# A state-space convolution kernel: table doublings on PSUM operands, tables laid out channel-innermost, K's operands turned first, and half of the first Toeplitz products ahead of the loop

## The reference

```
dtA = A * dt[:, None]                       # A = -exp(log_A_real) + 1j*A_imag, 64 modes per channel
Cs  = Cc * (exp(dtA) - 1.0) / A
K   = 2.0 * einsum('hn,hnl->hl', Cs, exp(dtA[:, :, None] * arange(2048))).real
mask = arange(2048) < length[:, None]
u_m = x * mask
y   = causal_convolution(u_m, K) + u_m * D[:, None]
out = x + y * mask
```

## Time and profile before

| what | value |
|---|---|
| median of 3 runs | 881.8 us (881.62 to 883.14) |
| the profiled execution's own time | 882.78 us |
| its span in the trace | 880.9 us |
| PE busy | 828.1 us, 94% |
| DVE busy | 755.0 us, 86% |
| POOL busy | 636.9 us, 72% |
| ACT busy | 624.6 us, 71% |
| mean DMA rate | 172 GB/s |

### The profile page before, as it was taken

One profiled execution on the slowest core, in us unless ns is written; L12 is line 12 of the kernel. 1 busy time (PEld: TensorE's weight loads), 2 busy tenths in 40 slices (PEclk: granted clock), 3 DMA queues, 4 the chain that ended last, 5 costly groups with the idle time before them and its releaser, 6 DMA issues.

```text
span 880.9 us, 22605 instructions
## 1 busy us (share of the span) xinstructions
PE 828.1 (94%) x6218; PEld 760.6 (86%) x6218; DVE 755.0 (86%) x2054; ACT 624.6 (71%) x1710; POOL 636.9 (72%) x692
## 2 busy tenths in 40 slices
PE   0377999999999999999999999999999999999997
PEld 0366988999988999999999999999999999999996
DVE  8976988888888888888888888888888888888886
ACT  2095767776767777777777777777777777777774
POOL 3727877777777877777787777777777778777771
PEclk9789999999999999999999999999999999999999
DMA  3002677777777777777777777777777777777775
GB/s 83 0 1 49 175 177 191 186 196 177 192 179 188 189 191 186 197 185 196 185 196 187 190 192 186 196 185 195 187 195 189 189 190 188 192 189 197 190 197 132
DMA packets 160947, 151.66 MB, mean 172 GB/s; under 512 B 13216, under 2 KB 160928, under 8 KB 160928
## 3 DMA queue, kind: packets, MB, share of 16 engines
q1 hardware_dynamic: 160928, 151.43, 67.8%
HBM read 84.08 MB, written 67.30 MB: 172 GB/s over the span
## 4 chain that ended last, share of the span: by engine, by line
PE 83%; DVE 5%; DMA 5%; ACT 2%; SPq 2%; POOL 1%; issue 1%; POOLq 0%; DVEq 0%
PE y L830 13%; PE y L832 13%; PE y L831 12%; PE y L865 12%; PE v L847 10%; PE xt_even L818 6%; PE xt_odd L818 6%; DMA xall<-in_x_dram 5%; PE v L830 3%; PE v L831 3%; PE v L832 3%; PE y L825 1%; PE y L826 1%; SPq L301 1%; ACT W L441 1%
## 5 line engine op out<-in xcount | busy, mean ns | idle before, releaser
L441 ACT ACTIVATE room<-v 64x192 f32<-64x192 f32 (+1 forms) x768 | 235.8, 307 | 173.6 <-DVE v L738 157.1
L738 DVE SCALAR_TENSOR_TENSOR v<-v,RV,mid 128x192 f32<-128x192 f32 (+2 forms) x512 | 192.4, 376 | 57.2 <-DVE mid L738 2.7
L738 DVE SCALAR_TENSOR_TENSOR mid<-room,RV,v 128x192 f32<-128x192 f32 (+2 forms) x512 | 184.2, 360 | 41.7 <-ACT room L441 22.2
L830 PE MATMUL y<-thi,uhi 128*128 128x256 f32 x512 | 186.4, 364 | 0.2 <-POOL tlo L409 0.2
L734 DVE COPY_PREDICATED xall<-mask,y 128x512 f32<-128x512 int32 x256 | 176.0, 736 | 1.4 <-issue 1.4
L830 PE MATMUL y<-fhi,zhi 128*128 128x256 f32 x512 | 154.6, 302 | 0.8 <-DVE zlo L564 0.7
L421 POOL TENSOR_TENSOR room<-W,B 128x512 f32 (+1 forms) x128 | 135.8, 1061 | 13.7 <-DVE W L708 13.6
L832 PE MATMUL y<-thi,ulo 128*128 128x256 f32 x512 | 144.5, 282 | 0.0
L832 PE MATMUL y<-fhi,zlo 128*128 128x256 f32 x512 | 144.0, 281 | 0.0
L831 PE MATMUL y<-tlo,uhi 128*128 128x256 f32 x512 | 144.0, 281 | 0.0
L831 PE MATMUL y<-flo,zhi 128*128 128x256 f32 x512 | 144.0, 281 | 0.0
(11 more groups left out here) (174 smaller groups left out, 1981.0 us busy)
## 6 DMA issues: line engine op xcount, KB each, us to landing
xall<-in_x_dram SPq DMA_DIRECT2D x256, 256.0 KB, 4.6
out_dram<-xall SPq DMA_DIRECT2D x254, 256.0 KB, 3.4
traw<-krows SPq DMA_DIRECT2D x128, 128.0 KB, 3.0
out_dram<-xall SPq DMA_DIRECT2D x4, 128.0 KB, 2.4
krows<-ksb SPq DMA_DIRECT2D x8, 16.0 KB, 1.8
cin<-in_L_cond_C_dram SPq DMA_DIRECT2D x1, 64.0 KB, 2.0
dall<-in_L_cond_D_dram SPq DMA_DIRECT2D x1, 64.0 KB, 2.4
krows<-zpad SPq DMA_DIRECT2D x1, 63.5 KB, 6.3
```

What stands on the lines that cost most here:

```text
L441: return act.activation(dst, src, ACT.Copy)
L738: return dve.scalar_tensor_tensor(out=out, in0=src, scalar=RV[:, h, k:k + 1], in1=other, op0=ALU.mult, op1=ALU.add)
L830: pe.matmul(o, a_hi, b_hi, start=start, stop=False, skip_group_check=True)
```

## The change

It touches the prologue, the layout of the tables and the first slot.

- `W1`, `W2`, `B1`, `B2`, `bsel` and `RV` become channel-innermost ([128, 16, 128] per plane). PSUM copies into them are contiguous; POOL's reads of them in the loop, for one channel at a time, have a step of 512 bytes. `Yk` is a new channel-first copy of the Y plane for K's products, turned in 4 extra steps.
- DVE's doublings take the powers from `turns`, a PSUM region that ACT fills (two copies), and two of the four temporaries are the PSUM banks `xt[0]` and `xt[1]`. `x_low(0, 0)` moves ahead of DVE's series, because `xt[0]` has to be free. `BANKS` becomes 5.
- The duplicates of NB's planes are copied by POOL instead of ACT.
- `STEPS` has K's operands first, then K, then B, X and R. D is added to K ahead of DVE's own table copies, and ACT's `NR` copies come behind its other table copies.
- ACT does `t_high(0)` first, DVE forms `tlo` of channel 0, and PE does the Toeplitz products of chunks 0 and 1 of channel 0 ahead of `turn_e(0)`. POOL's `t_low(0)` and those products in slot 0 go.

The core of the diff:

```diff
-BANKS = 6
+BANKS = 5
+STEPS = [("bsel", 8), ("bsel", 12), ("Yk", 8), ("Yk", 12), ("Y2", 8), ("Y2", 12), ("Y1", 8), ("Y1", 12),
+         ("Yk", 0), ("Yk", 4), ("bsel", 0), ("bsel", 4), ("Y1", 0), ("Y1", 4), ("Y2", 0), ("Y2", 4),
+         ("K", 0), ("K", 4), ("K", 8), ("K", 12),
+         ("B1", 8), ("B1", 12), ("B2", 8), ("B2", 12), ("B1", 0), ("B1", 4), ("B2", 0), ("B2", 4),
+         ("X1", 8), ("X1", 12), ("X2", 8), ("X2", 12), ("X1", 0), ("X1", 4), ("X2", 0), ("X2", 4), ("R", 0), ("R", 4)]
+BY_VECTOR = [STEPS.index(k) for k in [("B2", 4), ("X1", 12), ("X2", 12), ("X1", 4),
+                                          ("X2", 4), ("R", 0), ("R", 4)]]
...
-        W1 = sb("W1", [P, 2, H, SQ])
+        W1 = sb("W1", [P, 2, SQ, H])
...
+        turns = yb[1][1][:, 0:2 * 4 * N].rearrange("p (c k n) -> p c k n", c=2, n=N)
...
+            for n in range(2):
+                pool.tensor_copy(NB[:, half(n), 0, :], NB[:, half(n), 1, :]).then_inc(s_bdup, 1)
+                pool.tensor_copy(NB[:, half(n), 3, :], NB[:, half(n), 2, :]).then_inc(s_bdup, 1)
...
-                w1 = W1[:, :, h].unsqueeze(3).broadcast_to([P, 2, SQ, SQ])
+                w1 = W1[:, :, :, h].unsqueeze(3).broadcast_to([P, 2, SQ, SQ])
-                b1 = B1[:, h].unsqueeze(1).unsqueeze(1).broadcast_to([P, 2, SQ, SQ])
+                b1 = B1[:, :, h].unsqueeze(1).unsqueeze(1).broadcast_to([P, 2, SQ, SQ])
...
-                if exists(g, j, -2):
+                if exists(g, j, -2) and exists(g, j, -3):
                     t_low(*on(g, j, -2))
...
+            copy(turns[:, 0], lre[:, A_POW:A_POW + 4, :])
+            copy(turns[:, 1], lim[:, A_POW:A_POW + 4, :]).then_inc(s_turns, 1)
...
+            t_high(0, 0)
             e_high(0, 0)
...
+            x_low(0, 0)
             series(q, k, r, k)
...
-            temps = [q1, q2, q3, q4]
-            link(level(dve, link, NY, 1, 0, A_POW, temps, 0))
+            temps = [xt[0], q2, xt[1], q4]
+            coarse = [(turns[:, 0, k], turns[:, 1, k]) for k in range(4)]
+            link(level(dve, link, NY, 1, 0, coarse[0], temps, 0))
...
+            for t in range(T_K, T_K + 4):
+                dve.wait_ge(s_free[t % BANKS], t // BANKS + 1)
+            dve.tensor_tensor(k0, k0, dall[:].rearrange("p (g c) -> p g c", c=8), ALU.add).then_inc(s_kfin, 1)
+
+            for t in BY_VECTOR:
                 filled(dve, t)
                 dve.tensor_copy(place(t), four(t)).then_inc(s_free[t % BANKS], 1)
...
+            dve.wait_ge(s_thi, 1)
+            less(tlo[0][:], traw[0][:, ::-1], thi[0][:]).then_inc(s_tlo0, 1)
...
+                               Yk[:, 8 * g:8 * g + 8, :].rearrange("p c i -> p (c i)"),
+                               bsel[:, :, 8 * g:8 * g + 8].rearrange("p i c -> p c i"), start=True, stop=True)
...
+            for c in range(2):
+                toep_even(0, 0, c)
+                toep_odd(0, 0, c)
             turn_e(0, 0)
```

More of the change, by code:

```diff
@@ L87, in s4d_kernel @@
         q4 = sb("q4", [P, NPOW * N])
-        RV = sb("RV", [P, H, 8])
-        bsel = sb("bsel", [P, H, SQ])
+        RV = sb("RV", [P, 8, H])
+        bsel = sb("bsel", [P, SQ, H])
         tick = sb("tick", [P, 2])
@@ L166, in s4d_kernel @@
         s_nxp = sem("s_nxp")
+        s_turns = sem("s_turns")
+        s_tlo0 = sem("s_tlo0")
         s_yneg = sem("s_yneg")
@@ L247, in half, with level @@
             return slice(SQ // 2, SQ) if n == 0 else slice(0, SQ // 2)
-        def level(eng, link, table, re, im, first, temps, k, lo=0, hi=N):
+        def level(eng, link, table, re, im, turn, temps, k, lo=0, hi=N):
             m = 2 ** k
             old, new = slice(SQ - m, SQ), slice(SQ - 2 * m, SQ - m)
-            c, s = (t[:, first + k, lo:hi].unsqueeze(1).broadcast_to([P, m, hi - lo]) for t in (lre, lim))
+            c, s = (t[:, lo:hi].unsqueeze(1).broadcast_to([P, m, hi - lo]) for t in turn)
             rc, is_, rs, ic = (t[:, 0:(hi - lo) * m].rearrange("p (m n) -> p m n", m=m) for t in temps)
@@ L277, in place @@
                 return ksb[:, i:i + 4, :]
+            if table == "Yk":
+                return Yk[:, :, i:i + 4].rearrange("p h i -> p i h")
             whole = {"Y1": W1[:, 1], "Y2": W2[:, 1], "X1": W1[:, 0], "X2": W2[:, 0], "B1": B1[:], "B2": B2[:],
                      "bsel": bsel[:], "R": RV[:]}[table]
-            return whole[:, :, i:i + 4].rearrange("p h i -> p i h")
+            return whole[:, i:i + 4, :]
         block = ctx.enter_context(nc.Block())
@@ L395, in _ @@
             temps = [wide[:, a:a + part] for a in (0, part, 2 * npn, 2 * npn + part)]
-            level(pool, link, NX, 0, 1, A_POW, temps, 3, XSPLIT, N).then_inc(s_nxp, 1)
+            level(pool, link, NX, 0, 1, (lre[:, A_POW + 3], lim[:, A_POW + 3]), temps, 3, XSPLIT,
+                  N).then_inc(s_nxp, 1)
             for t in range(T_R - BANKS, T_R):
@@ L536, in slot @@
                     turn_odds(*one)
-                    t_high(*one)
+                    if has0:
+                        t_high(*one)
                 if has0:
@@ L888, in slot @@
                     turn_x(*two, 1)
-                if has0:
+                if has0 and exists(g, j, -1):
                     for c in range(2):
@@ L948, in _ @@
                 mm = pe.matmul(pro[t % BANKS][:, (g % 4) * P:(g % 4 + 1) * P],
[L949 to L950 removed]
+                               Yk[:, 8 * g:8 * g + 8, :].rearrange("p c i -> p (c i)"),
+                               bsel[:, :, 8 * g:8 * g + 8].rearrange("p i c -> p c i"), start=True, stop=True)
                 if g % 4 == 3:
                     mm.then_inc(s_fill[t % BANKS], 1)
+            pe.wait_ge(s_bdup, 2)
+            turn(T_K + 4, T_K + 7)
+            pe.wait_ge(s_bdup, 4)
+            turn(T_K + 8, T_K + 11)
+            pe.wait_ge(s_xneg, 1)
+            turn(T_K + 12, T_K + 15)
             pe.wait_ge(s_xneg, 2)
[L954 removed]
+            turn(T_K + 16, T_R - 1)
             pe.wait_ge(s_rot, 4)
```

104 lines of the change are left out of this document (42 added, 62 removed), and 4 rows, old and new, of the table STEPS.

## The result

| what | before | after |
|---|---|---|
| median (4 runs each, on one chip) | 882.47 us | 875.36 us (874.88 to 876.45) |
| profiled execution's own time, span | 882.78, 880.9 us | 875.22, 873.4 us |
| PE, DVE, ACT, POOL busy | 828.1, 755.0, 624.6, 636.9 us | 829.3, 744.0, 618.4, 725.0 us |

The ratio is 0.9921, with a 95% interval of 0.9904 to 0.9939. The changed kernel is faster, by 7.1 us where 13.5 were forecast. On two other chips the same kernel took 872.44 us (0.9886 [0.9866, 0.9906]) and 872.25 us (0.9894 [0.9875, 0.9913]), 9.1 and 9.6 us under its kernel before. All ratios are against the kernel before on the same chip; the spans of the second and third profiled executions are 869.9 and 868.3 us.

What follows compares the result with a forecast made beforehand. PE bounds the loop at 6.17 us a slot; only its start moves, 85.5 to 72.0, so the span goes from 880.9 to 867.4 and the median to 868.3 us. Own range 864.5 to 872; with second and third rival, to 877.5.

Steps and rivals of the forecast that it cites:

- S: The instant `from_state(0)` starts and PE runs without a gap; forecast at 72.0 instead of 85.5 us, 13.5 us earlier.
- the step on PSUM operands: DVE's doublings: one PSUM input ends the turns with POOL, so NY levels 0 to 2 take 4.78 instead of 14.84 us.
- the second rival: DVE's doublings: PSUM operands don't end the turns, NY keeps its time, S 8.9 us later than forecast, 877.2 us; chance 0.07.
- The sum behind the step: NY's 128x256 instruction: 0.42 us alone plus one POOL product of 1.06 make 1.48, so the two engines take turns.
- the limit of 1.67: POOL's slot in the loop: each of two products may grow from 1.06 to 1.67 us at no cost.
- The first rival: Loop: POOL's products, slowed by the 512-byte step, become the bound; 901 us at 1.80 a product, 967 at 2.12; chance 0.13.
- Do K's products hold this up?: Prologue: K ready at 47.1, 3.1 us before DVE; this slack covers `bsel`'s step, five banks and four extra steps.
- NB's products fall from 1.44 to 1.06: POOL's doublings in the prologue: free of turns, products take 1.06 us, so NB ends at about 39.
- Unless this costs PE over 75% more: K's products on PE: reading `bsel` with a 512-byte step stays within the 3.1 us slack below that extra cost.
- POOL starts at about 50.6 plus five table copies of DVE: Start of the loop on POOL: five copies of 0.60 us each put its start at 53.7.
- the wait for `traw` ... now sets the start: Ahead of `turn_e(0)`: `traw` lands at 59.1, `turn_e(0)` goes at 61.8, while POOL's `pf(0)` would allow 57.5.
- the third rival: Prologue: K's products over 75% slower, `combine` and `tlo` stuck behind POOL, or clock down; 3 to 6 us, 871.5 to 875; chance 0.12.

Runs made afterwards that it cites:

- the controls: The changed kernel measured again, unedited, on two other chips: 0.9886 (872.44 us) and 0.9894 (872.25 us) against the kernel before.
- Experiment 2: Changed kernel with `bsel` laid out channel-first again, so PE reads K's moving operand contiguously: 0.9864 against the kernel before.
- experiment 5: Changed kernel with 20 more transposes while PE waits for NB's end, 0.9892; separately with half the modes of NB's last level left out, 0.9906.
- experiment 4: Changed kernel without the 18 warm-up transposes, 0.9876; without early Toeplitz products, 0.9889; `NR` copies ahead of K's, 0.9877; early products behind `turn_e(0)`, 0.9892.
- experiment 6: Changed kernel with `bsel` contiguous, transposes ahead of NB's end and `NR` ahead of K, 0.9900; the same with 54 warm-up transposes instead of 18, 0.9881.
- experiment 7: Changed kernel with `bsel` contiguous, transposes ahead of NB, `NR` ahead of K, 26 warm-up transposes, Toeplitz products in slot 0, `t_high(0)`, `tlo` later: 0.9852, 869.71 us.
- experiment 1: Changed kernel with the temporaries and powers of DVE's doublings back in SBUF: 0.9971 against the kernel before.

## Why the prediction was right or wrong

**Right.** The loop's bound and the accounting by S held. So did the step on PSUM operands: NY from level 0 to `minus` took 37.7 - 27.4 = 10.3 us, as forecast, and undoing it costs 8.1 us of S at an equal clock, near the 8.9 of the second rival, which is refuted. The sum behind the step, 0.42 + 1.06 = 1.48, came out by luck: NB's products aren't the loop's, and alone they last 1.28 and not 1.06 us. The Trainium skill's surcharge for PSUM operands (VectorE: DVE Perf Modes, the TRN2 errata) would show as 65 ns an instruction. A product of 512 with its output and one input in PSUM lasts 0.68, as in SBUF, so the trace doesn't agree. From D's addition to `tlo` it took 64.0 - 54.3 = 9.7 us (forecast 9.9; at its end stand DVE's copies of R and not a turn behind POOL), from `turn_e(0)` to the end of `zlo` 10.1 (forecast 10.0). POOL's products took 1.40 us, under the limit of 1.67: a factor of 1.32, where I took 1.5. The rule of the Trainium skill (GPSIMD Engine Reference, Performance pitfalls for Q7 kernels) made 1.62 us of it, which the trace doesn't bear out. The first rival is refuted, by 0.53 us a slot. One of its sums was off: at 2.12 us a product it is 868.3 + 250 x 0.45 = 981 us, not 967.

**Where the miss lies.** `turn_e(0)` was forecast at 61.8 and came at 66.64 (64.95 in the controls). From there to S it took 10.3 us, forecast 10.2. So the whole miss is ahead of `turn_e(0)`.

**Wrong: "Do K's products hold this up?"** The prediction put K at 47.1, with 3.1 us of slack ahead of DVE's 50.2, and let that slack cover three unknowns. K came at 53.88, 6.8 us late, which is the slack and 3.7 us more:

- *NB's end, 39, was 41.6.* "NB's products fall from 1.44 to 1.06" took the duration of a product that reads broadcast rows for one that reads two whole streams. Alone these last 1.28 us. And 0.6 us is a shift that I gave to NY and not to NB: with `x_low(0, 0)` ahead of the series POOL's doublings begin later too, at 24.53 instead of 23.93. The trace of before had the nearer row, POOL's subtraction of two whole 512-element operands, free of turns: 1289 ns (the mean of 40, the number in front of the second bar).

```profile
L428 POOL TENSOR_TENSOR room<-room 128x512 f32<-128x512 f32 x40 | 51.6, 1289 | 9.3 <-POOL flo L404 9.3
```

- *The products of K, 4.8 us to the addition, were 7.9.* "Unless this costs PE over 75% more" was the condition. By its own record a matmul takes 395 ns instead of 275, 44% more, but the records overlap. In time on PE's queue the 32 products took 7.0 us instead of 3.6, 94% more. Experiment 2 shows the step as the cause.
- *The clock.* 1.7 us of the profiled execution, at 0.60 ahead of K. This was in the rivals for the early products only, not here. Its place differs from run to run of the same kernel (experiment 5).

The six steps themselves took 2.7 us at full clock where I had 3.3 for the copies, which gives 0.6 back. With a full clock ahead of K, D is added at 52.58, 2.0 late and not 3.7. DVE's own chain, free of K, would have ended at 52.2 (experiment 2): `combine` took 4.7 instead of 3.8 us, within its bounds, and `minus` waited 0.94 for POOL's share of NX, which I had called free.

**Wrong: "POOL starts at about 50.6 plus five table copies of DVE".** Those copies can't end before PE has turned what they copy. Sixteen steps of 0.44 us lie behind K on PE, from 52.9 to 60.1, so POOL starts at 61.0 (59.3 at full clock), not 53.7. Of the 7.3 us, K's lateness on PE is the larger part: had K left PE at 47.1, the sixteen steps would have ended at 54.1 (an estimate: 47.1 + 16 x 0.44). A second term was missing behind it: I put `pf(2)` 11.5 us after POOL's start, as before, with the old products; with three pairs of products of 1.40 us it is ready 13.5 us after it, and with `NR` early it is what PE waits for (experiment 4).

**Wrong: "the wait for `traw` ... now sets the start".** In the changed kernel `tlo` was ready at 64.0, and PE came at 65.40: PE's queue was the last, R's transposes behind `NR`, the copies of R, and 2.16 us of warm-up, which I had put "near 58" and outside the sum. Experiment 4 shows it from two sides. Without the warm-up PE waits 1.69 us for `tlo`, but DVE's copies of R stand in front of `tlo` there. Only in experiment 6, with three of PE's delays out, does `traw` end PE's wait, as predicted, and there S is at 77.56, for `tlo` comes at 63.5 instead of 60.5 and the clock falls. The 72.79 of experiment 7 is near the forecast's 72.0 by luck: that kernel has no wait for `traw` ahead of `turn_e(0)`. I had put as a sign against me that POOL's `pf` would end PE's gap. It was neither.

**What happened is the third rival**, "the start chain is longer than summed", 871.5 to 875, to which I gave 0.12; the 875.36 lies beyond the 872 of the forecast's own case and just beyond this rival's end, the 872.44 and 872.25 of the controls at its near end. Its parts (K's products, `combine`, the clock) were named one by one, and each was taken as unlikely because one slack covered it. They added up, and they shared that one slack with NB's end. The controls' S, 75.2, is 3.2 us behind the forecast, and the first measurement's, 76.9, is 4.9.

What stays open: why the loads of `x` make PE wait between none and 3.9 us, and what decides whether the lower clock is granted behind a pause of about 1 us. The 18 transposes took 2.16 us in the three executions of the changed kernel and in four other kernels, and 3.57 to 4.07 in five, after idle times of 1.03 to 1.20 us in all of them. Both are as large as most of the effects studied here.

## What to carry to other kernels

Where several unknown costs lie in one slack, add them before comparing with it, and walk the queue of every engine through the new order: the start here was PE's own list of transposes, not the longest wait. Take a duration for a new instruction from one that reads in the same way (broadcast or whole streams, contiguous or with a step), not from one of the same size. Taking a delay out of PE's way can cost what it gains when PE then idles, so fill such a gap with transposes up to the event that ends it, and not beyond: 54 of them ran 1.2 us past `tlo` (experiment 6), 20 of them 1.3 us past NB's end (experiment 7).

## What the runs showed of the hardware

- PE reads a float32 moving operand with a 512-byte step at 395 ns per 128x128 matmul instead of 275, 1.75 instead of 0.90 us for eight in a row.
- POOL, 512 float32 elements, two SBUF inputs, alone: 1.06 us where both are broadcast rows of 16, 1.40 where the same reads have a step of 512 bytes, 1.28 for two whole streams. Its copy of 512 takes 0.61.
- With DVE and POOL both on SBUF inputs, one DVE product of 256 and one POOL product of 512 repeat every 1.40 us (experiment 1), where alone they repeat every 0.34 and 1.24. The forecast's sum of 0.42 + 1.06 fits the 1.48 of DVE's record, but POOL's product isn't 1.06 alone, so a turn costs POOL 0.16 us and DVE 1.06. Why 1.06 and not 1.24 of POOL's product shuts DVE out wasn't tried. A single SBUF input is not always free of POOL: `minus`, which negates one SBUF plane into another, lasted 0.90 and 0.96 us beside POOL's doublings and 0.43 alone.
- After pauses of PE from about 1 to 3.8 us the granted clock was at the lower of its two levels, 1.2 GHz, for parts of the following stretch in some executions (0.60 from 43 to 46 us in the changed kernel's first, behind 2.72 us; 0.59 from 66 to 72 in experiment 6, behind 3.82 us), and at 2.4 GHz in the same stretch of others: the changed kernel's second and third have 1.00 from 43 to 46 us, and 0.50 and 0.62 from 34 to 38, where the first has 1.00.
